# Scores of the first tile of queries in one product of 512 columns, with the keys padded by heads in place of the queries

## What is computed

```python
x = x + 0.5 * ffn(layernorm(x), Wg, Wu, Wd)
x = x + attention(layernorm(x), w_q, w_k, w_v, w_o, rel_emb)   # 16 heads of 8, causal
x = x + 0.5 * ffn(layernorm(x), Wg, Wu, Wd)

def ffn(x):          # 8 experts, all summed, hidden width 512
    acc = 0
    for wg, wu, wd in zip(Wg, Wu, Wd):
        acc = acc + (silu(x @ wg) * (x @ wu)) @ wd
    return acc
# attention: rotary q and k; q = q / sqrt(8)
scores = einsum('bhqd,bhkd->bhqk', q, k) + einsum('bhqd,qkd->bhqk', q, rel)   # rel clipped at 32
attn   = softmax(where(causal, scores, -1e18))
ctx    = einsum('bhqk,bhkd->bhqd', attn, v) + einsum('bhqk,qkd->bhqd', attn, rel)
```

## Time and profile before

| | |
|---|---|
| median of 3 runs | 1435.46 us |
| the profiled execution's own time | 1438.3 us |
| its span | 1436.5 us |
| PE busy, matmuls | 1375.4 us, 8632 |
| DVE busy | 1278.3 us |
| ACT busy | 1101.9 us |
| POOL busy | 1087.4 us |
| mean granted TensorE clock | 0.994 |

### The profile page before, as it was taken

The page is one execution under the profiler, slowest core; times in us unless marked ns, Lnnn a source line. Parts: engine busy times, 40 slices in busy tenths (PEclk is TensorE's granted clock), DMA queues, the critical chain, the costliest instruction groups (busy, mean ns, idle before and its releaser), DMA issues.

```text
span 1436.5 us, 29572 instructions
## 1 busy us (share of the span) xinstructions
PE 1375.4 (96%) x8632; PEld 1076.9 (75%) x8632; DVE 1278.3 (89%) x2541; ACT 1101.9 (77%) x2642; POOL 1087.4 (76%) x956
## 2 busy tenths in 40 slices
PE   8999999999999999999999999999999999999898
PEld 7787676777777777777777778777777777778686
DVE  6887898999999999999999989899999999899565
ACT  6656778878778887788888878778887778788454
POOL 7967787787778877887778768787777877677555
PEclk9999999999999999999999999999999999999999
DMA  6404999999999999999999999899999999897200
GB/s 185 142 15 125 154 192 187 178 204 170 180 188 175 165 178 176 187 160 189 164 152 209 170 167 179 148 191 177 171 172 161 192 162 173 161 173 142 44 1 8
DMA packets 718386, 225.08 MB, mean 157 GB/s; under 512 B 652305, under 2 KB 697745, under 8 KB 718225
## 3 DMA queue, kind: packets, MB, share of 16 engines
q1 hardware_dynamic: 556224, 172.45, 72.9%
q10 hardware_dynamic: 162000, 50.75, 19.4%
HBM read 60.95 MB, written 69.86 MB: 91 GB/s over the span
## 4 chain that ended last, share of the span: by engine, by line
PE 47%; DVE 19%; ACT 9%; issue 7%; DMA 6%; ACTq 4%; SPq 4%; POOL 3%; POOLq 0%; DVEq 0%
PE work L708 9%; PE work L710 9%; PE work L709 9%; PE acc L786 5%; PE acc L787 4%; DVE hid L1071 4%; PE acc L791 4%; DMA probs_t<-probs 4%; DVE hid L1065 3%; DVE negmax L1167 3%; ACTq L1000 3%; PE work L839 3%; DVE work L1162 3%; ACT work L960 2%; DVE probs L1176 2%
## 5 line engine op out<-in xcount | busy, mean ns | idle before, releaser
L1218 POOL TENSOR_TENSOR hid_lo<-hid,hid_hi 128x512 fp32r<-128x512 f32 x512 | 663.5, 1302 | 215.6 <-ACT hid_hi L915 115.1
L909 ACT ACTIVATE hid<-work 128x512 f32<-128x512 f32 x512 | 310.1, 606 | 123.9 <-PE work L710 84.9
L1065 DVE SCALAR_TENSOR_TENSOR hid<-hid,work 128x512 f32<-128x512 f32 x512 | 345.7, 680 | 53.9 <-ACT hid L909 53.4
L1071 DVE TENSOR_TENSOR hid<-hid,work 128x512 f32<-128x512 f32 x512 | 346.6, 680 | 33.6 <-PE work L710 31.2
L915 ACT CAST hid_hi<-hid 128x512 fp32r<-128x512 f32 x512 | 320.1, 630 | 49.7 <-DVE hid L1071 30.8
L786 PE MATMUL acc<-hid_hi,wd 128*128 128x512 f32 x512 | 216.5, 423 | 12.4 <-ACT hid_hi L915 9.9
L1167 DVE TENSOR_REDUCE negmax<-work 128x1 f32<-128x384 f32 (+3 forms) x352 | 219.2, 634 | 1.2
L1233 POOL TENSOR_TENSOR probs<-exps,probs 128x512 f16<-128x512 f32 (+1 forms) x160 | 172.0, 1075 | 62.8 <-ACT probs L972 59.8
L708 PE MATMUL work<-xt,wg 128*128 128x512 f32 x512 | 207.0, 404 | 5.4 <-DVE xt L1040 1.5
L708 PE MATMUL work<-xt,wu 128*128 128x512 f32 x512 | 206.1, 402 | 2.8 <-DVE hid L1071 1.9
L791 PE MATMUL acc<-hid_lo,wd 128*128 128x512 f32 x512 | 204.1, 401 | 1.0 <-POOL hid_lo L1218 0.7
(11 more groups left out here) (97 smaller groups left out, 2184.5 us busy)
## 6 DMA issues: line engine op xcount, KB each, us to landing
prob_window_scratch<-probs SPq DMA_DIRECT2D x384, 80.0 KB, 3.5
rel_win<-rel_window_scratch ACTq DMA_DIRECT2D x250, 96.0 KB, 4.3
q_scratch<-rope SPq DMA_DIRECT2D x16, 512.0 KB, 4.2
qq<-q_scratch ACTq DMA_DIRECT2D x32, 256.0 KB
rel_window_scratch<-g_s SPq DMA_DIRECT2D x32, 256.0 KB, 5.1
k_scratch<-rope SPq DMA_DIRECT2D x16, 512.0 KB, 4.2
kk<-k_scratch ACTq DMA_DIRECT2D x32, 256.0 KB
prob_window_scratch<-probs SPq DMA_DIRECT2D x32, 256.0 KB, 3.2
```

Of the source, the lines that this page charges most:

```text
L909: act.activation(hid[:, arg % HB, :], work[bank_of["gate", arg]][:, :], ACT.Tanh, scale=0.5).then_inc(s_tanh, 1)
L1065: dve.scalar_tensor_tensor(out=hid[:, arg % HB, :], in0=hid[:, arg % HB, :], scalar=1.0, in1=work[bank_of["gate", arg]][:, :], op0=ALU.add ...
L1071: dve.tensor_tensor(hid[:, arg % HB, :], hid[:, arg % HB, :], work[bank_of["up", arg]][:, :], ALU.mult).then_inc(s_hid, 1)
L1218: pool.tensor_tensor(hid_lo[:, arg % 2, :], hid[:, arg % HB, :], hid_hi[:, arg % 2, :].bitcast(F32), ALU.subtract).then_inc(s_hlo, 1)
```

## The change

The four matmuls of 128 columns of a first tile (i = 0) become one of 512 columns. For that tile the padding takes the first 128 keys in place of the queries, so its 32 executions at i = 0 read kk and wait for the keys' load; the queries themselves are the weights, and the four padded copies of the keys are the moving part. The result has the same layout: 128 queries by four heads of 128 keys. Tiles 1 to 3 stay as they were. The scheduler learns of the new dependencies, and the rule falls that added 0.1 us to feed-forward steps behind scores of tiles 0 and 1 (after_short).

```diff
--- before.py
+++ after.py
@@ -242,7 +242,7 @@
                 begin = due[first_of(quad)]
                 step("ACT", 0.55, max(begin - 13, first - 13), "load_window", quad, ("qrel_store", gg),
                      ("prepare_lo", 5), ("near", last_of(quad - WB) if quad >= WB else None), lands=LATE)
-                step("POOL", 1.0, begin - 6, "q_pad", quad, ("load_q", gg),
+                step("POOL", 1.0, begin - 6, "q_pad", quad, ("load_q" if i else "load_k", gg),
                      ("scores", last_of(quad - 2) if quad >= 2 else None))
                 step("ACT", 0.3, due[last_of(quad)] + 5, "load_band", quad, ("store_band", last_of(quad)),
                      ("store_band", last_of(quad) - 1 if i else None), ("band_turn", back(gg, 1)),
@@ -266,7 +266,7 @@
             g, i, a = TASKS[k % NK]
             quad, columns = quad_of(k), HEADS[i] * (i + 1) * P
             step("PE", 0.01 * HEADS[i] + columns / 2350, due[k], "scores", k, ("q_pad", quad),
-                 ("load_k", quad // NT), done_with(back(k, 2)))
+                 ("load_q", quad // NT), ("load_k", quad // NT), done_with(back(k, 2)))
             step("DVE", 0.07 + HEADS[i] * (P if i == 0 else W) / (960 if i < 2 else 580), due[k] + 0.5, "near", k, ("scores", k),
                  ("load_window", quad))
             step("DVE", wide(columns), due[k] + 0.7, "largest", k, ("near", k))
@@ -302,7 +302,6 @@
     free = {"bank": [0.0] * BANKS, "rows": [0.0], "stats": [0.0]}
     tenant = [None] * BANKS
     bank_of, held_before, given, order = {}, {}, {}, []
-    after_short = False
     missing = {key: len(after) + len(before) for key, (*_, after, before) in steps.items()}
     followers = defaultdict(list)
     for key, (*_, after, before) in steps.items():
@@ -334,11 +333,9 @@
         assert start < math.inf
         name, arg = key
         _, takes, lands, *_ = steps[key]
-        if name in ("gate", "up", "down", "down_lo", "project") and (start > clock["PE"] or after_short):
+        if name in ("gate", "up", "down", "down_lo", "project") and start > clock["PE"]:
 
             takes += 0.1
-        if engine == "PE":
-            after_short = name == "scores" and TASKS[arg % NK][1] < 2
         open_steps[engine].remove((time, key))
         clock[engine] = start + takes
         given[key] = start + takes + lands
@@ -835,9 +832,15 @@
                         pe.wait_ge(s_kld[gg % 2], 16 * (gg // 2 + 1))
                     if places[0] == 0:
                         pe.wait_ge(s_qp, quad + 1)
-                    for n, a in enumerate(places):
-                        done = pe.matmul(bank[:, n * keys:(n + 1) * keys], q_pad[:, quad % 2, a, :],
-                                         kk[:, gg % 2, 0:keys], start=True, stop=True)
+                    if i == 0:
+
+                        pe.wait_ge(s_qld[gg % 2], 16 * (gg // 2 + 1))
+                        done = pe.matmul(bank[:, :], qq[:, gg % 2, 0:P], q_pad[:, quad % 2, :, :].rearrange(
+                            "p a k -> p (a k)"), start=True, stop=True)
+                    else:
+                        for n, a in enumerate(places):
+                            done = pe.matmul(bank[:, n * keys:(n + 1) * keys], q_pad[:, quad % 2, a, :],
+                                             kk[:, gg % 2, 0:keys], start=True, stop=True)
                     done.then_inc(s_sc, 1)
                 if name == "values":
                     gg, tiles = arg // VG, STAGES[arg % VG]
@@ -1257,12 +1260,15 @@
                 if name == "q_pad":
                     gg, i = arg // NT, arg % NT
                     if i == 0:
+                        pool.wait_ge(s_kld[gg % 2], 16 * (gg // 2 + 1))
+                    if i == 1:
                         pool.wait_ge(s_qld[gg % 2], 16 * (gg // 2 + 1))
                     if arg >= 2:
                         pool.wait_ge(s_sc, last_of(arg - 2) + 1)
                     shape = [P, HQ, P]
+                    source = (qq if i else kk)[:, gg % 2, i * P:(i + 1) * P]
                     pool.tensor_tensor(q_pad[:, arg % 2, :, :],
-                                       qq[:, gg % 2, i * P:(i + 1) * P].bitcast(F32)[:, None, :].to_broadcast(shape),
+                                       source.bitcast(F32)[:, None, :].to_broadcast(shape),
                                        rows[:, :, None].to_broadcast(shape), ALU.mult).then_inc(s_qp, 1)
 
 
```

## The result

The changed kernel takes 1450.38 us (median of 6 runs, 1446.48 to 1455.68), the kernel before 1434.33 us in the same comparison. The ratio is 1.011, with a 95% interval of 1.0078 to 1.0143: slower by 16 us. The forecast was 1445 within 1429 to 1460.

A forecast was written before the change was run, and what follows sets the result against it. TensorE (96% busy) and VectorE (89%), nearly full and in a fixed order, were taken as the bound. 1438.3 - 5.5 + 0.5 + 7 + 3.5 + 2.5 = 1446.3, less half of 2.8, gave 1445 us, range 1429 to 1460.

The forecast's parts named there:

- The order: Steps on all engines differ from unit 50 on; the largest term, costing 7 + 3.5 + 2.5 us.
- the products: One 512-column product for four at 32 first tiles: 6.7 us of TensorE time saved, 5.5 reaching the end.
- The hole at unit 224: First unit of pass 7: the accumulator copy waits for a norm's transposes of xn, stalling feed-forward; 7 us lost.
- VectorE has no room to catch up: At unit 224, gates and ups done in advance cannot be caught up on, VectorE being 94% busy.
- The 3 us for the clock: Upper-bound addition at unit 224: a granted clock of 0.50 behind the idle stretch, as at the last pass's start.
- The end of the attention: Last band product now behind the last two down_lo, so the last norm's statistics come later: 3.5 us, bounds 1 and 6.
- The rest of the order: Four more stretches of 13 or more steps between two downs, 0.6 us each: 2.5 us, bounds -5 and +10.
- The added wait: First paddings now need the keys and stand ahead of the first scores: 0.5 us, bounds 0 and 2.
- the 137: Sign at the first scores: a start later than 137 us would mean the added wait was priced too low.
- Rival 2: Short products stand where TensorE would soon wait for VectorE: nothing saved, holes paid, 1451.8 us; chance 0.07.
- Rival 1: Products count in full and holes close: 1434.8 us, or 1427.8 at its fast end; chance 0.42.
- Rival 3: The hole at unit 224 opens a run of them, attention lagging over 5 us further: about 1457; chance 0.13.

The follow-up runs named there:

- e2: Kernel before, with its four short products and padded queries, in the order and with the banks of the changed kernel: ratio 1.0101.
- e3: Kernel before with one added scheduler precedence: pass 6's copy of acc waits for the third sequence's third-norm transposes; order behind unit 220 rearranged: ratio 1.0026.
- e8: Kernel before with one place reordered: group 31's last attention steps and the last norm's statistics behind pass 14's last down_lo: ratio 1.0026.
- e4: Changed kernel with one more scheduler rule that keeps norms off xn until acc is copied, removing the hole at unit 224: ratio 1.0113.
- e6: Kernel before, old products kept, with only the paddings of quads 0 and 1 moved behind lo of unit 52: ratio 0.9995.
- e1: New products and paddings in the order and banks of the kernel before, first two paddings moved right behind the first keys' load: ratio 1.0067.
- three pairs: Three comparisons of new against old products, each pair in one same order: mean ratio difference +0.0003, 0.4 us, between -2 and +3.
- e9: Kernel before, own order, with each first tile's four short products computed twice: ratio 1.0054.
- e10: Kernel before, own order, with only the first of each first tile's four short products computed: ratio 0.9975.
- e5: New products in the order and banks of the kernel before, with the first two paddings moved behind lo of unit 52: ratio 1.0015.
- e7: Changed kernel with a searched table of scheduler shifts and the single product priced as one: 1430.34 us, ratio 0.9968 to the kernel before.
- e12: Changed kernel with a second table of scheduler shifts from a longer search: ratio 1.0045 to the kernel before.

## Why the prediction was right

**The direction was right, and by the reason given.** The order was named the largest term, 7 + 3.5 + 2.5 = 13 us. e2 measures it alone: 1.0101, 14.5 us (10.5 to 18.5).

**The closeness of the number was partly luck.** As a difference, the sum said 8 us (1438.3 to 1446.3), and 16 came. 5.5 of the missing 8 are the products, 1.5 the order, and the last one is within the noise. The forecast of 1445 still missed the measured 1450.4 by 5 only, because it started from 1438.3 less 1.4, and the median of before in the comparison is 1434.33, 2.6 us lower.

**The hole at unit 224** was put at 7 us, and at 14 us or more between two hi casts. The casts are 14.87 us apart, and the place loses 5.3 us in the changed kernel and 4.5 in e3. Two errors partly offset each other here. From down of 223 to hi of 226 I had 16 us; it is 19.7 (636.07 to 655.80), so the kernel comes out of the hole 12 us late and not 8. And more was caught up than I allowed for: "VectorE has no room to catch up" did not hold, since 7 of the 12 us are back by unit 240. The 3 us for the clock were the upper bound; the lower clock lasted 3.1 us here, not the 5 of the earlier trace rows.

**The end of the attention** was put at 3.5 us; it is 4.8 in the trace, and 3.7 in e8's ratio. The statistics came 4.3 us later rather than 3.5, and the transposes behind the longer wait took 1.09 us instead of 0.63.

**The rest of the order** was put at 2.5 us with wide bounds, 0.6 for each of four more stretches. What is left of 14.5 is 4.4 us, and the traces place it in front of the hole: the 5 us between units 96 and 192, 3 of them at unit 160, which was one of the four stretches. No run tests this place by itself. The three places make 15, what e2 measures within its interval. e4 shows how such costs move about: removing one hole let another open.

**The added wait** was put at 0.5 us. GpSimd waits 0.34 us for the first keys, the first scores start at 136.55 and so ahead of the 137 that I had set as a sign, and e6, with the paddings moved alone, is level with before. e1 shows what it would have been in a worse place.

**The products** were the step that failed in size: "What of it reaches the end? Between the chain's 47% (3.2 us) and all of it ... I take 5.5". TensorE's own saving was right, 0.23 us where 0.39 stood, 0.22 less for a block with its pair; what reaches the end is nothing that three pairs can show, at most 2 us. e9 and e10 put the worth of TensorE's time there at a half and a third. A third of 6.7 is 2.2 us, at the edge of what the pairs allow, so the 47% of the chain was nearer than my own weight. What takes the last 2 us was not settled. With 0 in place of 5.5 the sum is 1451.8, where 1450.4 was measured. Rival 2 named this case and got 0.07: of the stated times, 1451.8 is the closest. Its reason, that TensorE would soon have waited anyhow, is only half borne out, since e9 and e10 show that its time there is worth something.

I gave the 190 ns of a recorded weight load as the reason for the price of the short products. That number is not what a load costs in a row: four loads and products together step by 0.39 us. e10 is closer to the point: one short product alone is followed after 0.06 us, so the other three cost 0.11 each.

**Rival 1** (the products count in full, the holes close) is refuted by e2 and e5. Its fast end was also added up wrongly: 1438.3 - 8 + 0.5 + 2 + 1 - 5 is 1428.8, not 1427.8, so it does not reach the 1428.3 from which on I called it faster. **Rival 3** (a lag over 5 us that feeds itself, 1457) did not come: the last norm's statistics are 4.3 us further behind the last down than before, and behind the hole the trace gains a part back.

One caution on the single trace: the changed kernel's profiled execution is the fastest of its six, 8 us above the one of before while the medians differ by 16. It was quick in the front part: it reaches down of 223 at 636.07, e2 and e4 with the same order at 641.62 and 641.00, before at 635.49. So the distances within a stretch were compared, over several executions, and not the times from the start.

## What to carry to other kernels

Where a program lays out its own order, compare the orders before the products: count the work between two steps of the tightest chain, and look at who shares a buffer across a boundary. One such stretch was readable from the order to within 2 us of its cost, partly by errors that offset each other, while the saving that the change was about did not reach the end. To measure such a change, freeze the order and swap the form, then freeze the form and swap the order; without that its effect is drowned by orders whose times spread from 0.997 to 1.011 with the same work in them.

Ask the kernel's own scheduler as well, which costs no run; the prediction made no use of it. Its estimated end is 1375.5 us for the kernel before and 1396.4 for the changed one: 20.9 us later, where 16 were measured. For the other orders it says 11.5 later (e3, measured 3.7), 15.9 (e4, 16.2), 1.1 (e7, 4.6 faster) and 2.9 earlier (e12, 6.5 slower). It had the direction of the two large differences, and it is off by up to 9 us, so it cannot choose between near orders.

## What was not expected of the hardware

Time on a nearly full engine is worth less than its busy share says: with TensorE busy 96% of the span, 14 us more at the first tiles cost 7.7 us (e9; 4.6 to 10.9), 10.6 less gave 3.6 (e10; 0.4 to 6.6), and 6.7 less in one product in place of four gave none (between 3 us lost and 2 us saved). The first two intervals, as shares of what was added or taken, overlap; that the two directions differ is not shown.
